# A fused norm and quantised convolution: the weight load moves to ScalarE's queue, and the store of image 0 moves to SyncE's

## The chip, the cores and the metric

The kernel runs on one core of one Trainium2 chip. The metric is the device time of one execution in microseconds (us), as the median of several runs. A core has five engines that matter here: TensorE (PE in the profile), VectorE (DVE), ScalarE (ACT), GpSimd (POOL) and SyncE (SP), which only issues transfers in this kernel. Sixteen DMA engines move data between HBM and the on-chip memory SBUF. Transfers are issued from two places, SP and ACT, and each of the two has its own DMA queue: q1 in the profile is SP's, q10 is ACT's.

## What is computed

The input `x` has 32 images of 512 channels and 28 by 28 pixels in float32, 1.6 MB each. Each image is normalised per group of 16 channels (32 groups), quantised to 16 levels, multiplied with a quantised weight matrix per convolution group (four groups of 128 channels, permuted by one group), passed through an affine step and a ReLU, and added to both the normalised image and the image itself:

```python
def _L0_conv_ref(x, weight, lW, uW, lA, uA, gamma, beta, running_mean, running_var):
    identity = x
    xg = x.reshape(B, G, Cg, H, W)[:, perm]                 # perm = 1, 2, 3, 0
    xa = jnp.clip((xg - lA) / (uA - lA), 0.0, 1.0)
    xa = ste_round(xa * (ACT_LEVELS - 1)) / (ACT_LEVELS - 1)
    wq = ...                                                # the same for the weights, then (wq - 0.5) * 2
    y = jnp.einsum('bgihw,goi->bgohw', xa, wg).reshape(B, C, H, W)
    inv = gamma / jnp.sqrt(running_var + BN_EPS)
    y = y * inv[...] + (beta - running_mean * inv)[...]
    return jax.nn.relu(y) + identity

x = x + _L0_conv_ref(_gn(x), ...)       # _gn: group norm with 32 groups
```

## The kernel before

One image is one tile of 128 partitions by 4 convolution groups by 784 pixels. `images` is a ring of 12 such tiles (`RING`), and image n lives in slot n % 12 from its load to its store: the result is written over the image, and the store goes out from the same slot. So image n can only be loaded when the store of image n - 12 has landed, which the semaphores `stored[j]` tell.

The engines share an image as follows. DVE takes the statistics of two or three of its groups (line 460), ACT those of the rest (lines 236 and 242). PE averages them over the channels of a norm group, POOL makes the coefficients, ACT and POOL write the quantised levels (lines 270 and 424), DVE caps them (line 475), PE multiplies (line 604), POOL (and ACT for the last four images) applies the affine step to the image (lines 413 and 278), and DVE adds the product to it (`finish`, line 482), one group at a time. Each `finish` raises the semaphore `final` by one, so image n is ready for its store at 4n + 4. Statistics run five images ahead of the multiplication (`AHEAD`).

Every engine's program is written out by hand, in order. What bears on transfers:

- SP (line 188 on) loads image 0 in four pieces of one group each (392.0 KB), then the weights `w_raw`, then image 1 in four pieces, then images 2 to 31 whole. From image 12 on each load waits for `stored[j]` (line 198). After that it stores image 30, and image 31 in four pieces.
- ACT (line 218 on) issues two small loads of parameters at the start, and in its main loop the stores of images 0 to 29 (`store`, line 259), each at a fixed place among its activations. The store of image 0 stands behind the four quantisations and the copy of the mean that follow the statistics of image 5.
- DVE waits for `weights_in` (line 511) behind the statistics of image 0, then prepares the weights (lines 512 to 519), and only then takes the statistics of image 1.

Of the kernel before, what the change touches and what calls it, by code (L numbers as in the profile page):

```python
# [12 lines left out]
P = 128  # L13
# [6 lines left out]
RING = 12  # L20
PARTS = 3
AHEAD = 5
SINGLE = 2
HELPED = 4
ACT_STORES = 30
SETS = 3
SUBSETS = 4
DMA = 16


def fused_norm_quantised_conv(nc, x, weight, limits, channel_params, out):

    B, C, H, W = x.shape
# [44 lines left out]
    def output_group(g):  # L78
        return (g + G - 1) % G

    with ExitStack() as ctx:
        def sb(name, shape, dtype):
            return ctx.enter_context(nc.sbuf_tensor(name, shape, dtype))
# [4 lines left out]
        def sem(name):  # L88
            return ctx.enter_context(nc.semaphore(name))
# [25 lines left out]
        w_raw = sb("w_raw", [P, G, P], F32)  # L115
# [30 lines left out]
        weights_in = sem("weights_in")  # L146
# [40 lines left out]
        @block.sync  # L187
        def _(sync):
            for n in range(SINGLE):
                for g in (0, G - 1, 1, 2):  # L190
                    sync.dma_start(images[:, n, g], x_v[n][:, g]).then_inc(first_loaded[n][g], DMA)
                if n == 0:
                    sync.dma_start(w_raw[:], weight.rearrange("(g o) i -> o g i", o=P)).then_inc(weights_in, DMA)

            def load(n):
                j = n % RING
                if n >= RING:
                    sync.wait_ge(stored[j], DMA * (n // RING))
                sync.dma_start(images[:, j], x_v[n]).then_inc(x_loaded[j], DMA)

            def store(n):
                sync.wait_ge(final, G * n + G)
                sync.dma_start(out_v[n], images[:, n % RING]).then_inc(stored[n % RING], DMA)

            for n in range(SINGLE, B):
                load(n)
            for n in range(ACT_STORES, B - 1):
                store(n)
            for g in range(G):
                o = output_group(g)  # L210
                sync.wait_ge(final, G * (B - 1) + g + 1)
                sync.dma_start(out_v[B - 1][:, o], images[:, (B - 1) % RING, o]).then_inc(stored[(B - 1) % RING], DMA)
            for j in range(RING):
                stores = len(range(j, B, RING)) + (G - 1 if j == (B - 1) % RING else 0)
                sync.wait_ge(stored[j], DMA * stores)

        @block.scalar
        def _(act):
            act.dma_start(rows[:], channel_params.rearrange("k (g p) -> (k g) p", p=P)).then_inc(rows_in, DMA)
            act.dma_start(limit_row[:], limits).then_inc(limits_in, DMA)  # L220
            act.wait_ge(eps_done, 1)
            nc.scalar.activation(early[:], eps[:, 0:1], ACT.Sqrt, bias=eps[:, 1:2])
            act.wait_ge(cols_turned, 1)
# [33 lines left out]
                nc.scalar.activation(std[:], var_ps[:, 0:2 * G], ACT.Sqrt, bias=eps[:, 0:1]).then_inc(std_done, 1)  # L257

            def store(n):
                if 0 <= n < ACT_STORES:  # L260
                    act.wait_ge(final, G * n + G)
                    act.dma_start(out_v[n], images[:, n % RING]).then_inc(stored[n % RING], DMA)

# [38 lines left out]
            for n in range(-1, B - 1):  # L302
                m = n + AHEAD
                if n % 2:
                    u = (n + 3) // 2
                    for g in range(quant_on_act(n + 2) if n + 2 < B else 0):
                        quantise(n + 2, g)
                        if g == 0 and u < PAIRS:
                            copy_mean(u)
                    store(n - 1)  # L310
                    if m < B:
                        image_sums(m)
                    if u < PAIRS:
                        deviation(u)
                    if m < B:
                        image_squares(m)
                    for g in range(G - affine_on_act(n + 1), G):
                        affine(n + 1, g)
                else:
                    for g in range(G - affine_on_act(n + 1), G):  # L320
                        affine(n + 1, g)
                    if m < B:
                        image_stats(m)
                    store(n - 1)
                    for g in range(quant_on_act(n + 2) if n + 2 < B else 0):
                        quantise(n + 2, g)
# [329 lines left out]
```

## Time and profile before

| | us |
|---|---|
| median of three runs | 258.81 (258.80 to 259.05) |
| the profiled execution, its own time | 258.41 |
| the span that its profile shows | 256.7 |
| DVE, ACT, POOL and PE busy | 230.0, 215.2, 212.0, 193.9 |

The span runs from the first to the last record of the profile; 1.7 us of the execution lie outside it. The page of the profile gives the busy time of each engine, and, in 40 slices of the span, how busy the DMA engines were and how many GB/s they moved. The views used further on are: the busy times by stretch (with the mean rate of the DMA engines), the DMA view (what each queue moved in a stretch, and how long the transfers issued there took to land), the instructions in order of time, and the waits. In the views in order of time, `SPq` and `ACTq` are the sequencers that issue transfers; a long duration there means that the issue was held up.

### The profile page before, as it was taken

To read this page: it belongs to the slowest core of one execution; us is meant where nothing else is said; L and a number is where in the kernel's file an instruction comes from. 1 tells how busy PE (TensorE), PEld (TensorE's weight loads), DVE (VectorE), ACT (ScalarE), POOL (GpSimd) and SP (SyncE) were. 2 spreads that over 40 slices of the span, in tenths; PEclk is the share of its full clock that TensorE was granted. 3 is DMA by queue.
4 is the path that set the end of the run, shared out by engine and by line. 5 is a ranking of instruction groups with operands and counts; after the bars stand their busy time and mean duration, and the time that the engine had idled before them with its cause. 6 is when DMAs were issued, how large, how long until landed. Compare 5 with 4: busy or idle time off the path is not lost.

```text
span 256.7 us, 3463 instructions
## 1 busy us (share of the span) xinstructions
PE 193.9 (76%) x999; PEld 109.3 (43%) x999; DVE 230.0 (90%) x363; ACT 215.2 (84%) x394; POOL 212.0 (83%) x340
## 2 busy tenths in 40 slices
PE   1142996969889888979797997877696969889920
PEld 0132644435454444445443554343444435454510
DVE  2898698999999999999999899999999999969940
ACT  4437898999999999989999889999899888999300
POOL 6126869999999999999999999999999999999100
PEclk9999999797979798988979599999979797979995
DMA  6999999999999999999999999999999999999994
GB/s 225 398 411 411 408 409 406 418 416 417 418 414 418 417 416 418 411 418 416 416 415 416 418 416 413 419 417 415 417 413 418 416 418 409 402 400 402 393 399 193
DMA packets 34516, 103.25 MB, mean 402 GB/s; under 512 B 1202, under 2 KB 1730, under 8 KB 34498
## 3 DMA queue, kind: packets, MB, share of 16 engines
q1 hardware_dynamic: 18624, 54.86, 53.8%
q10 hardware_dynamic: 15874, 48.18, 47.0%
q8 instruction: 8, 0.13, 0.2%
q14 instruction: 10, 0.08, 0.1%
HBM read 51.65 MB, written 51.38 MB: 401 GB/s over the span
## 4 chain that ended last, share of the span: by engine, by line
POOL 52%; DVE 16%; issue 11%; PE 9%; ACT 5%; DMA 2%; DVEq 0%; SPq 0%; POOLq 0%; ACTq 0%
POOL images L413 27%; POOL levels L424 8%; DVE images L482 7%; PE prod L604 6%; DVE stats L460 4%; POOL dev L375 3%; DVE codes L475 3%; PE var_ps L584 3%; POOL dev L378 2%; DMA images<-in_x 2%; POOL scaled L404 2%; ACT levels L270 2%; POOL coef L406 2%; POOL norm L402 1%; ACT unused L242 1%
## 5 line engine op out<-in xcount | busy, mean ns | idle before, releaser
L604 PE MATMUL prod<-codes,w_t 128*128 128x392 bf16 x768 | 160.8, 369 | 7.9 <-DVE codes L475 2.9
L482 DVE SCALAR_TENSOR_TENSOR images<-prod,floor,images 128x784 f32<-128x784 f32 x128 | 128.0, 1019 | 8.5 <-PE prod L604 8.2
L413 POOL TENSOR_SCALAR images<-images,coef 128x784 f32<-128x784 f32 x120 | 123.7, 1042 | 0.0
L604 PEld LDWEIGHTS prod<-codes,w_t 128*128 128x128 bf16 x768 | 79.1, 110 | 81.6 <-issue 24.6
L270 ACT ACTIVATE levels<-images,coef 128x784 int16<-128x784 f32 x95 | 91.3, 1028 | 1.1 <-issue 1.1
L460 DVE BATCH_NORM_STATS2 stats<-images 128x6 f32<-128x392 f32 x136 | 68.9, 551 | 5.4 <-DMA images<-in_x 5.4
L236 ACT ACTIVATE unused<-images 128x784 bf16<-128x784 f32 x60 | 50.7, 847 | 7.5 <-DMA images<-in_x 5.2
L242 ACT ACTIVATE unused<-images,sums 128x784 bf16<-128x784 f32 x60 | 56.1, 939 | 0.1
L475 DVE TENSOR_SCALAR codes<-levels 128x3136 bf16<-128x3136 int16 x32 | 34.7, 1085 | 1.0 <-ACT levels L270 0.7
L584 PE MATMUL var_ps<-dev,avg 128*128 128x8 f32 x128 | 19.6, 280 | 20.0 <-POOL dev L382 20.0
L424 POOL TENSOR_SCALAR levels<-images,coef 128x784 int16<-128x784 f32 x33 | 33.6, 1020 | 0.1
L584 PEld LDWEIGHTS var_ps<-dev,avg 128*128 128x128 f32 x128 | 18.6, 221 | 25.4 <-POOL dev L382 25.2
L375 POOL TENSOR_TENSOR dev<-stats,gmean 128x16 f32<-128x16 f32 (+1 forms) x16 | 10.9, 682 | 9.6 <-ACT gmean L250 9.6
L575 PE MATMUL mean_ps<-sums,avg 128*128 128x4 f32 (+1 forms) x32 | 6.5, 274 | 12.2 <-DVE sums L468 12.2
L575 PEld LDWEIGHTS mean_ps<-sums,avg 128*128 128x128 f32 x32 | 5.2, 203 | 17.2 <-DVE sums L468 12.2
L242 ACT ACTIVATION_READ_ACCUMULATOR unused<-images,sums 128x1 f32 x60 | 11.4, 190 | 0.0
L236 ACT ACTIVATION_READ_ACCUMULATOR unused<-images 128x1 f32 x60 | 11.3, 188 | 0.0
L256 ACT ACTIVATE half_var<-var_ps,eps 128x8 f32<-128x8 f32 x16 | 4.2, 265 | 6.7 <-PE var_ps L584 6.4
L398 POOL TENSOR_TENSOR newt<-rough 128x8 f32<-128x8 f32 x16 | 3.9, 242 | 5.5 <-DVE rough L492 5.5
L250 ACT ACTIVATE gmean<-mean_ps 128x8 f32<-128x8 f32 x16 | 2.7, 170 | 6.1 <-PE mean_ps L576 6.0
L278 ACT ACTIVATE images<-images,coef 128x784 f32<-128x784 f32 x8 | 7.7, 1032 | 0.0
L404 POOL TENSOR_TENSOR scaled<-norm,coef_mul 128x32 f32<-128x32 f32 x16 | 6.5, 409 | 1.2
(66 smaller groups left out, 83.2 us busy)
## 6 DMA issues: line engine op xcount, KB each, us to landing
images<-in_x SPq DMA_DIRECT2D x30, 1568.0 KB, 14.5
out<-images ACTq DMA_DIRECT2D x30, 1568.0 KB, 18.8
images<-in_x SPq DMA_DIRECT2D x8, 392.0 KB, 6.6
out<-images SPq DMA_DIRECT2D x1, 1568.0 KB, 8.8
out<-images SPq DMA_DIRECT2D x4, 392.0 KB, 7.4
w_raw<-in_weight SPq DMA_DIRECT2D x1, 256.0 KB, 6.5
rows<-in_channel_params ACTq DMA_DIRECT2D x1, 8.0 KB, 2.3
limit_row<-in_limits ACTq DMA_DIRECT2D x1, 0.0 KB
```

The lines of the kernel that those rows point to most:

```text
L236: nc.scalar.activation(unused[:, g % 2], images[:, n % RING, g], ACT.Identity, scale=1.0 / HW, accum_out=sums[:, u % 2, 0, j, g:g + 1]).th ...
L242: nc.scalar.activation(unused[:, g % 2], images[:, n % RING, g], ACT.Square, scale=-1.0, bias=sums[:, u % 2, 0, j, g:g + 1], accum_out=sum ...
L270: nc.scalar.activation(levels[:, n % 2, g], images[:, n % RING, g], ACT.Relu, bias=coef[:, u % 2, 1, 0, G * j + g:G * j + g + 1], scale=co ...
L375: nc.gpsimd.tensor_tensor(dev[:, :, 0:k], stats[:, par, :, 0:k, :, 1], mean[:, :, 0:k].to_broadcast([P, 2, k, SUBSETS]), ALU.subtract)
L413: nc.gpsimd.tensor_scalar(here, here, coef[:, u % 2, 0, 1, G * j + o:G * j + o + 1], coef[:, u % 2, 1, 1, G * j + o:G * j + o + 1], ALU.mu ...
L424: nc.gpsimd.tensor_scalar(levels[:, n % 2, g], images[:, n % RING, g], coef[:, u % 2, 0, 0, G * j + g:G * j + g + 1], coef[:, u % 2, 1, 0, ...
L460: nc.vector.bn_stats(two, images[:, n % RING, g, h * HALF:(h + 1) * HALF]).then_inc(bn_done, 1)
L475: nc.vector.tensor_scalar(codes[:, n % 2], levels[:, n % 2], 0.0, TOP, ALU.max, ALU.min).then_inc(capped, 1)
L482: nc.vector.scalar_tensor_tensor(out=two, in0=prod[:, k % SETS, :, 0:HALF], scalar=floor[:, o:o + 1], in1=two, op0=ALU.max, op1=ALU.add).t ...
L575: nc.tensor.matmul(mean[:, :, 0:k], avg[:], sums[:, par, 0, :, 0:k], start=True, stop=True)
L584: done = nc.tensor.matmul(var, avg[:], dev2[:, :, :, s], start=False, stop=(s == SUBSETS - 1))
L604: done = nc.tensor.matmul(prod[:, k % SETS, h, 0:HALF], w_t[:, part, output_group(g)], codes[:, n % 2, g, h * HALF:(h + 1) * HALF], start= ...
```

## The change

Two transfers change their place.

- The load of the weights leaves SP's program, where it stood between the four pieces of image 0 and the four of image 1. It becomes the third transfer that ACT issues, ahead of ACT's first activation.
- The store of image 0 leaves ACT's loop. SP issues it, behind the load of image 11 and ahead of the load of image 12, which is the first that waits for this very store.

```diff
@@ block.sync
             for n in range(SINGLE):
                 for g in (0, G - 1, 1, 2):
                     sync.dma_start(images[:, n, g], x_v[n][:, g]).then_inc(first_loaded[n][g], DMA)
-                if n == 0:
-                    sync.dma_start(w_raw[:], weight.rearrange("(g o) i -> o g i", o=P)).then_inc(weights_in, DMA)
...
-            for n in range(SINGLE, B):
+            for n in range(SINGLE, RING):
+                load(n)
+            store(0)
+            for n in range(RING, B):
                 load(n)
             for n in range(ACT_STORES, B - 1):
                 store(n)
@@ block.scalar
             act.dma_start(limit_row[:], limits).then_inc(limits_in, DMA)
+            act.dma_start(w_raw[:], weight.rearrange("(g o) i -> o g i", o=P)).then_inc(weights_in, DMA)
             act.wait_ge(eps_done, 1)
...
             def store(n):
-                if 0 <= n < ACT_STORES:
+                if 0 < n < ACT_STORES:
                     act.wait_ge(final, G * n + G)
```

SP's program from its start, before. `images<-in_x` of 128x784 is one group of an image, of 128x4x784 a whole image; `stored0` is the semaphore of slot 0.

```order
L191 DMA images<-in_x 128x784 x4
L193 DMA w_raw<-in_weight 128x4x128
L191 DMA images<-in_x 128x784 x4
L199 DMA images<-in_x 128x4x784 x10
L199 DMA images<-in_x 128x4x784 [waits stored0]
L199 DMA images<-in_x 128x4x784 [waits stored1]
```

The same place after:

```order
L191 DMA images<-in_x 128x784 x8
L197 DMA images<-in_x 128x4x784 x10
L201 DMA out<-images 128x4x784 [waits final]
L197 DMA images<-in_x 128x4x784 [waits stored0]
L197 DMA images<-in_x 128x4x784 [waits stored1]
```

The weights are gone from between images 0 and 1, and a store that waits for `final` stands between the ten unconditional loads and the first load that waits for a slot.

ACT's program around the first two stores, before (images 6 and 7 are those whose loads it waits for):

```order
L250 ACTIVATE gmean<-mean_ps 128x8 [waits coef_done,mean_done]
L270 ACTIVATE levels<-images,coef 128x784 x2
L262 DMA out<-images 128x4x784 [waits final]
L236 ACTIVATE unused,sums<-images 128x784 [waits dev_done,var_done,squared,x_loaded6]
```

and after:

```order
L252 ACTIVATE gmean<-mean_ps 128x8 [waits coef_done,mean_done]
L272 ACTIVATE levels<-images,coef 128x784 x2
L238 ACTIVATE unused,sums<-images 128x784 [waits dev_done,var_done,squared,x_loaded6]
```

The store of image 0 with its wait is gone from there, and ACT's first store is now that of image 1, at its old place behind the statistics of image 7.

## Rows read from the trace of the kernel before

**Rows 1.** The page: the engines, the DMA engines in 40 slices, HBM traffic.

```profile
PE 193.9 (76%) x999; PEld 109.3 (43%) x999; DVE 230.0 (90%) x363; ACT 215.2 (84%) x394; POOL 212.0 (83%) x340
...
DMA  6999999999999999999999999999999999999994
GB/s 225 398 411 411 408 409 406 418 416 417 418 414 418 417 416 418 411 418 416 416 415 416 418 416 413 419 417 415 417 413 418 416 418 409 402 400 402 393 399 193
...
HBM read 51.65 MB, written 51.38 MB: 401 GB/s over the span
```

**Rows 2.** Busy time of each engine by stretch; the last column is the DMA rate.

```profile
4.00:6.50 2.50, 0.69 (x3) 0.60 (x3) 1.82 (x9) 1.24 (x4) 1.30 (x3) 1.00 0.96 306
8.00:40.00 32.00, 18.43 (x79) 12.37 (x79) 27.58 (x57) 22.48 (x43) 16.74 (x31) 1.00 1.03 410
45.00:60.00 15.00, 12.99 (x69) 7.21 (x68) 14.97 (x24) 14.47 (x30) 14.45 (x22) 0.86 1.03 417
60.00:200.00 140.00, 118.56 (x622) 65.57 (x620) 136.31 (x211) 133.37 (x251) 133.99 (x201) 0.89 1.03 416
216.00:240.00 24.00, 21.63 (x118) 11.72 (x117) 21.74 (x28) 23.21 (x33) 21.43 (x31) 0.92 1.03 402
240.00:248.00 8.00, 4.99 (x30) 2.53 (x27) 6.93 (x8) 0.00 (x0) 0.00 (x0) 1.00 1.01 392
```

**Rows 3.** DMA view, 40.2 to 43.7: what each queue moved.

```profile
q1 hardware_dynamic: 464, 1.41, 102.0%
q8 instruction: 1, 0.02, 1.9%
```

**Rows 4.** DMA view, 62 to 200: what each queue moved.

```profile
q10 hardware_dynamic: 9473, 28.81, 51.9%
q1 hardware_dynamic: 9372, 28.49, 51.2%
```

**Rows 5.** In order of time: SP's issues (start, duration, line, count).

```profile
2.64 0.43 SPq L193 DMA_DIRECT2D w_raw<-in_weight  x1
...
5.85 31.53 SPq L199 DMA_DIRECT2D images<-in_x  x10
...
33.52 3.86 SPq L199 DMA_DIRECT2D images<-in_x  x1
...
53.13 0.37 SPq L199 DMA_DIRECT2D images<-in_x  x1
...
60.76 0.37 SPq L199 DMA_DIRECT2D images<-in_x  x1
...
200.81 0.37 SPq L199 DMA_DIRECT2D images<-in_x  x1
```

**Rows 6.** Waits of SP's queue: us in total, times, longest.

```profile
SPq L199 <- DMA out<-images: 156.1, 20, 15.7
SPq L203 <- DVE images L482: 42.0, 1, 42.0
```

**Rows 7.** In order of time: ACT's issues of stores 0, 1, 2, 3.

```profile
40.18 0.42 ACTq L262 DMA_DIRECT2D out<-images  x1
...
49.01 0.40 ACTq L262 DMA_DIRECT2D out<-images  x1
...
54.47 0.38 ACTq L262 DMA_DIRECT2D out<-images  x1
...
62.82 0.38 ACTq L262 DMA_DIRECT2D out<-images  x1
```

**Rows 8.** DMA view: issued in 36 to 44 (load 11, store 0), size, us to landing.

```profile
images<-in_x SPq DMA_DIRECT2D x1, 1568.0 KB, 26.8
out<-images ACTq DMA_DIRECT2D x1, 1568.0 KB, 12.9
```

**Rows 9.** DMA view: load 31, issued at 200.81.

```profile
images<-in_x SPq DMA_DIRECT2D x1, 1568.0 KB, 13.7
```

**Rows 10.** In order of time, the start: DVE and ACT behind the first loads.

```profile
7.32 2.07 DVE L460 BATCH_NORM_STATS2 stats<-images 128x6 f32<-128x392 f32 x4 [1.41 <-DMA images<-in_x]
9.31 0.53 DVE L512 TENSOR_SCALAR w_rest<-w_raw,cols,w_rng 128x512 f32<-128x512 f32 x1
12.05 2.90 DVE L460 BATCH_NORM_STATS2 stats<-images 128x6 f32<-128x392 f32 x6
...
17.08 0.86 ACT L236 ACTIVATE unused<-images 128x784 bf16<-128x784 f32 x1 [0.54 <-DMA images<-in_x]
...
21.00 0.86 ACT L236 ACTIVATE unused<-images 128x784 bf16<-128x784 f32 x1 [0.47 <-DMA images<-in_x]
...
36.03 1.03 DVE L482 SCALAR_TENSOR_TENSOR images<-prod,floor,images 128x784 f32<-128x784 f32 x1
```

**Rows 11.** In order of time, the end: ACT's issues and image 31, DVE's last group.

```profile
208.40 3.91 ACTq L262 DMA_DIRECT2D out<-images  x1
...
212.49 0.86 ACT L236 ACTIVATE unused<-images 128x784 bf16<-128x784 f32 x1 [1.05 <-issue]
...
216.54 0.86 ACT L236 ACTIVATE unused<-images 128x784 bf16<-128x784 f32 x1
...
241.20 5.73 DVE L482 SCALAR_TENSOR_TENSOR images<-prod,floor,images 128x784 f32<-128x784 f32 x6
```

**Rows 12.** DMA view, 248 to 256.7: rate in 40 slices, and the last piece stored.

```profile
GB/s 418 389 418 389 404 418 361 433 389 433 361 418 404 389 375 418 433 404 332 317 332 288 274 245 187 144 144 58 87 58 58 14 29 29 0 0 0 0 0 0
...
out<-images SPq DMA_DIRECT2D x1, 392.0 KB, 8.8
```

## The prediction

> **What bounds the kernel now.** I read the page first, and on it the line of the DMA engines: they are 90% busy or more in every slice but the first and the last, at about 400 to 419 GB/s [rows 1]. DVE is 90% busy too, ACT and POOL a little less, so the next question is which of the two would be missed. The DMA view answers it: the last piece of image 31 is issued at about 247, right behind DVE's last group (241.20 + 5.73 = 246.9) [rows 11], and takes 8.8 us to land, with the DMA engines at their full rate until about 252 [rows 12]. So a queue of stores, some 5 us deep, stands between the last computed group and the end. The bytes are the same before and after (51.65 MB read, 51.38 MB written [rows 1]). The time is therefore start + bytes / rate + tail, and a change to the order of transfers counts only through the rate, through an idle stretch of the DMA engines, or through compute that comes more than the depth of that queue later.
>
> The table by stretch shows that the rate has levels [rows 2]: 410 GB/s while only loads run (8 to 40), 416 to 417 while loads and stores run side by side (45 to 200), 402 while only stores run (216 to 240). In the side by side stretch the two queues share evenly: 9,473 packets of ACT's against 9,372 of SP's [rows 4]. So what I have to work out is how many images are moved in each of the three manners.
>
> **The change, part 1: the weights.** They cost the same bytes on either queue. On SP the issue takes 0.43 us [rows 5], but SP is far ahead of the DMA engines (it is soon held up at its issues: 31.5 us for the ten loads from 5.85 on [rows 5]), so those 0.43 us buy nothing. On ACT they delay its first activation by about as much; ACT has nothing to do before image 0's second piece, so that is free. What moves is the order of arrival. The weights now share with the pieces of image 0, instead of coming behind them. 0.26 MB at 410 GB/s are 0.64 us, so the pieces that DVE waits for at 7.32 come by 0 to 0.64 us later, and its preparation of the weights (9.31) and the statistics of image 1 (12.05) follow [rows 10]: DVE was without a gap from 7.32 on, so nothing absorbs it. It could also be less than nothing if the weights came long before 9.31 and DVE's wait at 7.32 were unchanged, but then the pieces still have to be worked off in the same order. I take +0.6 us for the computation. On the path that sets the end this is worth 0: the 5 us of queued stores hide it, less about 2 us that a last piece needs by itself (1 us of transfer, 392 KB at 402 GB/s, and an allowance of 1 us to start), so 3 us of cover. If that cover were gone, the 0.6 us would count in full.
>
> **Part 2: the store of image 0.** Before, ACT issues it at 40.18 [rows 7], though its last group was finished at 37.06 (36.03 + 1.03) [rows 10]. Until 43.7 ACT's queue moves nothing [rows 3]; then it shares with loads. It lands at 53.1 (40.2 + 12.9 [rows 8]), and SP, which had waited for it for 15.7 us [rows 6], issues load 12 at 53.13 [rows 5]. After, SP comes to this store when it is done with issuing load 11, at 33.52 + 3.86 = 37.4 [rows 5], finds it ready (or within the 0.6 us of part 1), and puts it **behind** loads 9, 10 and 11 in the same queue. So an earlier issue gives a later transfer. Loads come every 3.92 us while they are alone (images 2 and 3 at 17.08 and 21.00 [rows 10]), so load 11 now lands at 21.0 + 8 x 3.92 = 52.4, where before it landed at 60.3 (33.5 + 26.8 [rows 5, 8]). Only then come stores, and meanwhile ACT has issued store 1 (49.0) and soon store 2 (54.5), both at their old places [rows 7]. Store 0 and store 1 share the engines: two images at 402 GB/s are 8.0 us, so store 0 lands at about 60.5, 7 us later than before. Load 12 goes out then, and load 13 right behind it (before: 60.76 [rows 5]). With the allowance of 1 us to start and some for landing, loads and stores run side by side again from about 62. Until then store 2 keeps the engines at work: stores 0, 1 and 2 are 12 us of work from 52.4 on, to 64.4. So I count no idle stretch.
>
> Now the three manners. Before: loads alone until 43.7, which leaves (52.4 - 43.7) / 3.92 = 2.2 images; 9.8 are loaded alone, 22.2 side by side with as many stores, and 9.8 are stored alone. That fits the trace: load 31 lands at 200.8 + 13.7 = 214.5 [rows 5, 9], and 9.8 x 3.99 us more give 253.6. After: 12 are loaded alone, 20 side by side; stored alone are 32 - 20 = 12 (2.4 of them between 52.4 and 62, 9.6 at the end). So 2.2 pairs leave the fast manner for the two slow ones. One image is 1.606 MB, 2.2 are 3.53 MB, and they cost 3.53 x (1/410 + 1/402 - 2/416) ms per GB = **+0.42 us**. With the ends of the slices on the page that are of one manner (406 to 411 for loads, 400 to 403 for stores, 415 to 417 beside each other) this is 0.3 to 0.6 us. It could be below nothing only if the DMA engines lost something in the shared stretch that they don't lose alone, and the rates say the opposite.
>
> A rule of the Trainium skill ("DMA: Bandwidth & Descriptors", section "Issuing engines are not separate DMA queues") says that transfers started on several engines run on the same 16 DMA engines and interleave, so that more issuers save only the time of issuing. By that rule alone the whole change would be worth nothing.
>
> **Part 3: what the later loads do to the computation.** 20 pairs at 7.72 us (3.21 MB at 416 GB/s) from 62 on bring load 31 at 216.4, 1.9 us later than before. ACT took image 31 at 216.54 [rows 11], 2.0 us after it landed, and itself comes 0.6 us later now. Here a stall of ACT may shrink as well: it stood for 1.05 us before 212.49 because a store's issue was held up for 3.91 us [rows 11]. I count 0, and at most 1 us, under the 3 us of cover. Early in the run there is no need of image 12 for a long time after 70.
>
> **The sum.** 258.41 (this execution's own time) + 0.42 + 0 + 0 = 258.83. The profiled execution is 0.40 us under the median of the three runs, 258.81; on the median's scale that is 259.23, and I say 259.2. For a verdict, 0.2% is about what a measurement of this kernel can tell from no change, which is 0.52 us: below 258.29 is faster, above 259.33 slower. The forecast lies just inside the upper edge.
>
> **Rivals.**
>
> *Rate levels that don't follow the manner.* The 402 of the end and the 410 of the start may belong to those parts of the run (the ring being filled, the last images) rather than to loads or stores being alone. Then the moved pairs cost nothing: 258.8, the same. For it: all of the rows for one manner are from one end of the run. Against it: the rate goes up within the 20 us around 43.7, and down just where load 31 has landed [rows 1, 2]. The rule of the Trainium skill above would give this time. Chance 0.18.
>
> *The DMA engines run dry around 62 (slower).* SP stands in line for the store of image 0, and loads 12 and 13 with it, 7 us longer than before. As long as ACT's stores 1 and 2 are in the queue, nobody misses them. It decides if store 0 lands after about 63.4, or if store 2 is issued later than about 60 in place of 54.5: from there each us is lost in full, since the bytes are still to be moved. The same wait makes all later loads late; from 5 us on (2.0 of slack at image 31, 3 of cover) the computation too would reach the end. The place where I can be off is store 0's landing, which I have from two images of work; an uneven split of the engines of 2 to 3 us would bring it about. Price some 1 to 1.5 us: 260.3. Chance 0.15.
>
> *The start or the end gets better (faster).* From 4.0 to 6.5 the engines moved only 306 GB/s, though 96% busy [rows 2]. That costs 2.5 x (1 - 306 / 410) = 0.63 us against the stretch after. If this comes from eight small loads and the weights on one queue, the move could give it back. And from 240 to 248 the rate is 392 in place of 402, 0.2 us, because stores came a little late there; an ACT that is held up less could fill that. Both together against the cost: 259.23 - 0.83 = 258.4, and with the first rival's rates 258.0. Against it: the weights came only behind the slow stretch (issued at 2.64, used at 9.31 [rows 5, 10]), so they can hardly be its cause. Chance 0.17, of which 0.12 under 258.29.
>
> *That the change doesn't do what it says* is no case by itself: by my count the store of image 0 is indeed not sooner, and that is in the forecast.
>
> **How the numbers follow.** Forecast 0.50, from 258.8 to 259.8 by the bounds 0.3 to 0.6 and the scatter of the runs (258.80 to 259.05); 0.30 of it under 259.33 and 0.20 over. With the rivals: faster 0.12, same 0.30 + 0.18 + 0.05 = 0.53, slower 0.20 + 0.15 = 0.35. The range goes from 258.3, where only the faster case is left out, to 260.3.
>
> **What the profile after would show.** SP's store of image 0 issued near 37.4 to 41 and landing near 60.5; ACT's queue empty until about 50; load 12 issued at about 60.5 and load 13 right behind; two stretches of stores alone, 52 to 62 near 402 GB/s and again from about 216; load 31 landing near 216; image 1's statistics on DVE at about 12.6. I am wrong in the size if the rate in 52 to 62 is 410 or more, wrong in the mechanism if store 0 shares with loads before 50, and the slower rival holds if a slice near 62 falls under 390. If the end moves with the computation and not with the bytes, then the 3 us of cover were a misreading.

## The result and the profile after

The change makes the kernel slower: median 260.34 us of 22 runs against 258.72 us for 22 runs of the kernel before taken beside them. The ratio is 1.0052, with a 95% interval of 1.0041 to 1.0062, so about +1.35 us (1.1 to 1.6). On the scale of the 258.81 us shown ahead of the prediction this is 260.2. The two medians lie 1.6 us apart, a little more than the ratio on record gives; all prices below go by such ratios and their intervals. The spans of the two profiled executions, 258.8 and 256.7 us, lie 2.1 us apart. Of all runs of the experiments one, of 343.9 us (e6), was in a slow state and is left out.

The page after, its parts 1 and 2, to be read against [rows 1]:

```profile
PE 195.6 (76%) x999; PEld 110.8 (43%) x999; DVE 228.2 (88%) x363; ACT 215.1 (83%) x394; POOL 212.6 (82%) x340
...
DMA  6999999999999999999999999999999999999995
GB/s 225 399 413 412 409 410 407 406 401 319 382 416 414 417 417 416 415 416 417 418 414 416 417 418 417 415 417 416 415 414 417 418 414 412 401 399 401 399 400 210
...
HBM read 51.65 MB, written 51.38 MB: 398 GB/s over the span
```

The bytes are the same. The first seven slices and those from the twelfth on differ by 4 GB/s at most, but for the 38th and the last, which are fuller than before. The eighth and ninth (406 and 401 in place of 418 and 416) show what was forecast, loads alone and then stores alone. The tenth and the eleventh do not: 319 GB/s where it had 417, and 382 where it had 418. The share of busy time of the DMA engines, as a digit, hides this: it is 9 in both. The table by stretch for the same kernel places the loss (columns as in [rows 2], the DMA share and rate last):

```profile
58.00:60.00 2.00, 1.89 (x15) 1.46 (x15) 2.00 (x3) 1.75 (x3) 1.60 (x5) 1.00 0.73 282
62.00:64.00 2.00, 1.71 (x10) 0.60 (x7) 2.00 (x4) 2.00 (x6) 1.95 (x2) 1.00 0.97 256
64.00:67.00 3.00, 1.20 (x7) 0.54 (x8) 3.00 (x6) 2.91 (x9) 2.26 (x7) 1.00 1.03 414
68.00:76.00 8.00, 6.06 (x37) 3.64 (x38) 7.97 (x13) 7.85 (x14) 7.92 (x10) 0.97 1.02 387
216.00:240.00 24.00, 22.48 (x119) 12.60 (x120) 22.87 (x32) 21.78 (x35) 22.34 (x35) 0.87 1.03 402
240.00:248.00 8.00, 7.51 (x45) 3.97 (x42) 8.00 (x10) 3.87 (x5) 2.93 (x4) 1.00 1.03 398
```

At 58 to 60 the DMA engines really lack work (share 0.73, 282 GB/s). At 62 to 64 they are busy and move only 256 GB/s. Against 401 (stores alone), 409 and 416 GB/s this is 2 x 0.30 = 0.6 us, 2 x 0.37 = 0.75 us, and 8 x 0.07 = 0.56 us from 68 to 76: 1.9 us in these three stretches. The DMA view of 40 to 80 gives the whole loss in bytes, the kernel before first:

```profile
DMA packets 5440, 16.61 MB, mean 415 GB/s; under 512 B 154, under 2 KB 154, under 8 KB 5437
DMA packets 5104, 15.58 MB, mean 390 GB/s; under 512 B 146, under 2 KB 146, under 8 KB 5101
```

1.03 MB are missing, which is 2.5 us at 416 GB/s, the forecast's own term among them. Up to 40 us and from 80 to 216 us both kernels move the same to within 0.02 MB. The end, on the other hand, is a little fuller than before: 398 in 240 to 248, where [rows 2] had 392. So the span is 2.1 us longer.

What led there, in order of time. The start on DVE, which stands against [rows 10], and the issue of the weights:

```profile
1.79 0.40 ACTq L222 DMA_DIRECT2D w_raw<-in_weight  x1
...
8.98 1.04 DVE L462 BATCH_NORM_STATS2 stats<-images 128x6 f32<-128x392 f32 x2 [0.17 <-DMA images<-in_x]
11.37 0.55 DVE L514 TENSOR_SCALAR w_rest<-w_raw,cols,w_rng 128x512 f32<-128x512 f32 x1 [1.35 <-DMA w_raw<-in_weight]
11.95 0.43 DVE L515 TENSOR_SCALAR w_rest<-w_rest 128x512 f32<-128x512 f32 x1
...
14.13 1.96 DVE L462 BATCH_NORM_STATS2 stats<-images 128x6 f32<-128x392 f32 x4
```

The weights are issued 0.85 us earlier and are used at 11.37 in place of 9.31: DVE waits for them for 1.35 us. The statistics of image 1 begin at 14.13 in place of 12.05, so the computation is 2.1 us late. About 0.6 us of that comes from the pieces of image 0 (DVE is done with them at 10.0 in place of 9.4), the rest from the wait for the weights. The DMA view gives the transfer itself 9.6 us to land, where it had 6.5:

```profile
w_raw<-in_weight ACTq DMA_DIRECT2D x1, 256.0 KB, 9.6
```

Then the stores. SP's issues of store 0, of load 12 and of load 13, and ACT's of stores 1 and 2 (against [rows 5, 7]):

```profile
39.42 2.96 SPq L201 DMA_DIRECT2D out<-images  x1
...
58.83 0.37 SPq L197 DMA_DIRECT2D images<-in_x  x1
...
61.45 0.37 SPq L197 DMA_DIRECT2D images<-in_x  x1
```

```profile
51.85 0.41 ACTq L264 DMA_DIRECT2D out<-images  x1
58.26 0.39 ACTq L264 DMA_DIRECT2D out<-images  x1
```

Store 0 takes 19.4 us to land, at 58.8, and load 12 goes out at 58.83, 5.7 us later than before. Store 2 goes out at 58.26, 3.8 us later than before. From about 54 on each queue has one store to work off, store 0 on SP's and store 1 on ACT's. The DMA view of 57 to 58 and of 58 to 60 shows how they run out (packets, MB, and the time that the packets took as a share of the 16 engines'):

```profile
q10 hardware_dynamic: 124, 0.39, 99.9%
q1 hardware_dynamic: 4, 0.01, 3.3%
...
q10 hardware_dynamic: 193, 0.56, 72.6%
q1 hardware_dynamic: 2, 0.00, 0.4%
```

Nearly all of store 0 has been moved by 57, but load 12 waits for its last packets until 58.8. The DMA engines that are through with stores 0 and 1 have nothing to do in the meantime. Load 12 doesn't move at once when it is issued either: from 58.9 to 62.5 SP's queue moves no packet.

### The profile page after: what moved, and what is told of

Its sections match the earlier page's. It is cut to its first block, busy times and chain, and to the rows that moved or that the text cites. A ratio compares the mean times of both kernels' runs of the same rounds, so it can differ in the third digit from the quotient of the medians.

```text
span 258.8 us, 3463 instructions
## 1 busy us (share of the span) xinstructions
PE 195.6 (76%) x999; PEld 110.8 (43%) x999; DVE 228.2 (88%) x363; ACT 215.1 (83%) x394; POOL 212.6 (82%) x340
## 4 chain that ended last, share of the span: by engine, by line
POOL 43%; DVE 26%; PE 12%; issue 11%; DMA 4%; DVEq 0%; ACTq 0%; ACT 0%; POOLq 0%
POOL images L415 22%; DVE images L484 13%; PE prod L606 8%; POOL levels L426 7%; DVE stats L462 6%; DVE codes L477 5%; PE var_ps L586 4%; DMA w_raw<-in_weight 4%; POOL dev L380 3%; POOL dev L377 2%; POOL coef L408 2%; POOL newt L400 1%; POOL dev L384 1%; POOL scaled L406 1%; POOL newt L401 1%
## 5 line engine op out<-in xcount | busy, mean ns | idle before, releaser
L415 POOL TENSOR_SCALAR images<-images,coef 128x784 f32<-128x784 f32 x120 | 129.7, 1091 | 0.0
L477 DVE TENSOR_SCALAR codes<-levels 128x3136 bf16<-128x3136 int16 x32 | 32.9, 1027 | 0.7 <-ACT levels L272 0.4
L426 POOL TENSOR_SCALAR levels<-images,coef 128x784 int16<-128x784 f32 x33 | 32.7, 993 | 0.1
L586 PE MATMUL var_ps<-dev,avg 128*128 128x8 f32 x128 | 21.2, 293 | 13.8 <-POOL dev L384 13.8
L586 PEld LDWEIGHTS var_ps<-dev,avg 128*128 128x128 f32 x128 | 20.7, 242 | 18.2 <-POOL dev L384 17.8
L377 POOL TENSOR_TENSOR dev<-stats,gmean 128x16 f32<-128x16 f32 (+1 forms) x16 | 7.3, 457 | 12.4 <-ACT gmean L252 12.4
L380 POOL TENSOR_TENSOR dev<-sums,gmean 128x16 f32<-128x16 f32 (+1 forms) x16 | 8.7, 542 | 0.0
L613 PE MATMUL prod<-ident,w_raw 128*128 128x128 f32 x4 | 1.1, 434 | 9.5 <-DVE w_raw L520 9.5
```

The lines of the kernel that those rows point to most:

```text
L377: nc.gpsimd.tensor_tensor(dev[:, :, 0:k], stats[:, par, :, 0:k, :, 1], mean[:, :, 0:k].to_broadcast([P, 2, k, SUBSETS]), ALU.subtract)
L380: nc.gpsimd.tensor_tensor(dev[:, :, k:G], own[:, :, k:G].to_broadcast([P, 2, G - k, SUBSETS]), mean[:, :, k:G].to_broadcast([P, 2, G - k, ...
L415: nc.gpsimd.tensor_scalar(here, here, coef[:, u % 2, 0, 1, G * j + o:G * j + o + 1], coef[:, u % 2, 1, 1, G * j + o:G * j + o + 1], ALU.mu ...
L426: nc.gpsimd.tensor_scalar(levels[:, n % 2, g], images[:, n % RING, g], coef[:, u % 2, 0, 0, G * j + g:G * j + g + 1], coef[:, u % 2, 1, 0, ...
L477: nc.vector.tensor_scalar(codes[:, n % 2], levels[:, n % 2], 0.0, TOP, ALU.max, ALU.min).then_inc(capped, 1)
L586: done = nc.tensor.matmul(var, avg[:], dev2[:, :, :, s], start=False, stop=(s == SUBSETS - 1))
```

## The experiments

Each kernel was timed beside the kernel before on the same chip; ratios are to those runs. One count of 0.1% is 0.26 us.

**One half at a time.** e1 has the weights on ACT's queue and the store of image 0 at its old place:

```diff
-                if n == 0:
-                    sync.dma_start(w_raw[:], ...).then_inc(weights_in, DMA)
...
             act.dma_start(limit_row[:], limits).then_inc(limits_in, DMA)
+            act.dma_start(w_raw[:], ...).then_inc(weights_in, DMA)
```

> Half of the change: the weights on ScalarE's queue, the store of image 0 where it was. Theory (two parts that need each other): the weights land late (11.3 in place of 9.1), so the whole computation comes 2 to 3 us later, but the queue of stores at the end covers it, and stores mix with loads from about 46: 258.7 to 259.3, +0.0 to +0.5 us on before. The DMA rate has no slice under 400 in the middle. Rival (the late weights cost by themselves, because the end follows the computation): +1.3 us or more, near the full change.

Measured: 259.17 us, ratio 1.0027 (1.0006 to 1.0048), +0.7 us. The middle value is above the +0.0 to +0.5 expected, but the interval (0.2 to 1.2) takes in much of that range; the rival's +1.3 lies just outside. There is no gap in the middle (412 GB/s in 45 to 60, 416 from 60 to 200); most of the loss is near the end:

```profile
230.00:240.00 10.00, 9.72 (x49) 4.95 (x49) 7.91 (x10) 9.82 (x13) 9.35 (x15) 0.85 0.96 374
240.00:248.00 8.00, 7.12 (x42) 3.98 (x43) 8.00 (x10) 3.65 (x4) 2.17 (x2) 1.00 0.88 342
```

e2 has only the store on SP, behind load 11:

```diff
-            for n in range(SINGLE, B):
+            for n in range(SINGLE, RING):
+                load(n)
+            store(0)
+            for n in range(RING, B):
                 load(n)
...
-                if 0 <= n < ACT_STORES:
+                if 0 < n < ACT_STORES:
```

> The other half: the store of image 0 on SyncE behind load 11, the weights where they were. Theory: computation in time, store 2 issued at about 54.5, so the DMA engines have work until load 12 comes; the only cost is that about two pairs of load and store no longer run side by side: +0.3 to +0.6 us on before, and no slice near 60 under 390 GB/s. Rival (the store behind the loads drains the DMA engines by itself): +1.3 us or more and a slice near 320 GB/s at 58 to 62, as in the full change.

Measured: 259.50 us, ratio 1.0042 (1.0024 to 1.0061), +1.1 us. By the middle values the store is the larger half, though the intervals of e1 and e2 overlap, and it costs more than twice my term for it. The interval (0.6 to 1.6) doesn't leave out the rival's +1.3. The profiled run of e2 is its fastest (258.79 of 258.79 to 260.79), and it has no dip: 401 GB/s at 58 to 60, 409 at 62 to 64, 406 at 64 to 67. So this one run looks as I had forecast, and the other nine are slower.

**Is it the delay that the weights bring, or their packets?** e3 is e2, and e5 the kernel before, each with DVE's first operation on the weights repeated:

```diff
             dve.wait_ge(weights_in, DMA)
-            chained(nc.vector.tensor_scalar(w_rest[:], w_raw[:], bounds[:, 0:1], w_rng[:, 1:2], ALU.subtract, ALU.mult))
+            for _ in range(5):
+                chained(nc.vector.tensor_scalar(w_rest[:], w_raw[:], bounds[:, 0:1], w_rng[:, 1:2], ALU.subtract, ALU.mult))
```

> The store on SyncE as in the change, weights at their old place, and VectorE's first operation on the weights done five times in place of once (the same values; 4 x 0.55 = 2.2 us more ahead of the statistics of image 1). Theory: what the weights' new place does is to delay the computation, nothing else, so this gives the full change's time, +1.2 to +2 us on before, store 2 is issued near 57 to 58 and the DMA engines have a slice of 320 to 360 GB/s near 58 to 60. Rival (the weights' packets on the other queue cost DMA time or disturb the order of the engines): the time of the store alone, +0.3 to +0.6.

> The kernel before, both transfers at their old places, with VectorE's first operation on the weights done five times in place of once: 2.2 us of delay to the computation and nothing else. The weights alone on ScalarE's queue (e1) gave +0.7 us. Theory (late weights act through the delay of the computation alone, and the stores queued at the end cover less than I had counted): the same, +0.4 to +1.2 us, with slices of 350 to 390 GB/s among the last five. Rival (3 us of cover hold, and e1's loss is from the weights' packets): no change, the last slices at 400.

Measured: e3 260.29 us, ratio 1.0066 (1.0046 to 1.0086); e5 259.12 us, ratio 1.0022 (1.0005 to 1.0040). The delay in the place of the weights' move gives what the move gives: e5 beside e1 (1.0022 and 1.0027), e3 beside the full change (1.0066 and 1.0052), within the intervals. In e3 store 2 went out at 57.41, as expected, but the slow stretch came at 62 to 64 (351 GB/s) and not at 58 to 60 (400). e5 loses at the end as e1 does:

```profile
230.00:240.00 10.00, 9.93 (x49) 5.01 (x49) 7.71 (x10) 9.86 (x13) 9.53 (x15) 0.83 0.96 375
240.00:248.00 8.00, 7.04 (x42) 3.94 (x43) 8.00 (x10) 3.60 (x4) 2.25 (x2) 1.00 0.88 343
```

374 and 375, 342 and 343: the same picture at the end, which speaks for the weights acting through the late computation. In the middle the two runs differ: e5 has 375 and 358 GB/s at 60 to 64, where e1 has 412 and 416. How late the computation is at the end, DVE's last groups tell (before 241.20 [rows 11]; here after the change, in e1 and in e5):

```profile
243.71 5.73 DVE L484 SCALAR_TENSOR_TENSOR images<-prod,floor,images 128x784 f32<-128x784 f32 x6
244.90 5.73 DVE L481 SCALAR_TENSOR_TENSOR images<-prod,floor,images 128x784 f32<-128x784 f32 x6
244.98 5.73 DVE L482 SCALAR_TENSOR_TENSOR images<-prod,floor,images 128x784 f32<-128x784 f32 x6
```

In e1 and e5 image 1's statistics began 2.9 and 2.7 us late (14.90 and 14.72), and the last groups 3.7 and 3.8 us late. That is more than the 3 us of cover that I had counted, and it is over by about what the runs cost, 0.7 and 0.6 us. After the change it is 2.5 us, and there the end is full. So these runs don't refute 3 us of cover. The DMA engines do lose 10 x (1 - 375 / 402) + 8 x (1 - 343 / 402) = 1.8 us of work on average from 230 to 248, and the end moves by 0.6. That would fit engines of unequal progress, of which those ahead run dry while the last one still has stores queued. This reading is an inference; the view doesn't tell the engines apart.

**Do the rates follow the manner?** e4 computes nothing; it moves `x` through the 12 tiles to the output in phases, so its output is `x`: loads alone, stores alone, loads alone again, then both together, then the last stores.

> No computation at all, only transfers of x through the ring of 12 tiles to the output (the output is x): 12 loads alone, 12 stores alone, 12 loads alone, then 12 stores beside 8 loads, and the last 8 stores. Theory (the rate follows the manner): about 410 GB/s in both stretches of loads alone, 402 in the stores alone in the middle of the run, 416 side by side. Rival (the rate follows the part of the run): the middle stretches all at 416, or all the same.

Measured (264.62 us; here columns are stretch, POOL, clock, DMA share, rate):

```profile
8.00:45.00 37.00, 0.00 (x0) 1.00 1.03 411
60.00:96.00 36.00, 0.00 (x0) 1.00 1.03 404
108.00:145.00 37.00, 0.00 (x0) 1.00 1.03 411
172.00:210.00 38.00, 0.00 (x0) 1.00 1.03 418
222.00:250.00 28.00, 0.00 (x0) 1.00 1.03 404
```

Loads alone 411 at the start and in the middle, stores alone 404 in the middle and at the end, together 418. The rate follows the manner and not the part of the run: the first rival of the prediction is out. It isn't a matter of two queues being at work either: after the change, from 53 to 57, both queues carry stores alone (278 packets of ACT's, 250 of SP's) at 402 GB/s.

**How much of it is the computation?** In e6, e7 and e8, DVE's statistics of images 8 to 31 read 56 columns in place of 392, so the output rests on a part of the data; DVE has much less to do from 57 us on, and nothing changes ahead of that. e6 is the kernel before, e7 is e2, e8 the full change.

```diff
-                nc.vector.bn_stats(two, images[:, n % RING, g, h * HALF:(h + 1) * HALF]).then_inc(bn_done, 1)
+                cols_read = 56 if n >= 8 else HALF
+                nc.vector.bn_stats(two, images[:, n % RING, g, h * HALF:h * HALF + cols_read]).then_inc(bn_done, 1)
```

> The kernel before with VectorE's statistics of images 8 to 31 read over 56 columns in place of 392 (so these statistics, and the output, are of a part of the data): about 40 us less work on VectorE from 57 us on, nothing changed ahead of that. Theory: the kernel before is bound by the transfers, with up to 0.3 us lost at the end where stores come late: -0.2 to -0.8 us. Rival (the computation bounds it): several us faster.

> The store of image 0 on SyncE (as e2), with the same light statistics from image 8 on. Against e6 this is the price of the store's new place in the transfers alone, since the end can't be held up by the computation. Theory: +0.3 to +0.6 us on e6, from two pairs less side by side. Rival (part of e2's +1.1 us is a late computation at the end): if e7 is +1.1 us on e6 as well, it is not.

> The full change with the same light statistics from image 8 on. Against e7: what the late weights do to the transfers, by way of the stretch at 58 to 60 in which the DMA engines run dry (319 GB/s in that slice of the full change), the end being covered. Theory: the bytes not moved there are lost, +0.8 to +1.6 us on e7. Rival (what is lost there is only time that fast DMA engines would have waited at the end anyway): within 0.4 us of e7.

| | median | ratio to before | interval |
|---|---|---|---|
| e6, before with light DVE | 258.94 | 0.9998 | 0.9985 to 1.0011 |
| e7, store on SP with light DVE | 259.89 | 1.0040 | 1.0023 to 1.0056 |
| e8, full change with light DVE | 259.90 | 1.0035 | 1.0020 to 1.0050 |

e6 shows that DVE doesn't bound the kernel before: with much less work it gives nothing that can be told, where 0.2 to 0.8 us had been expected. Together with e4, which has the same rates without any computation, it leaves the transfers as the bound. e7 against e6 is 0.42%, as e2 against before and more than the +0.3 to +0.6 us expected: the store's price needs no late computation at the end. e8 against e7 is nothing, against my expectation of +0.8 to +1.6. But e8 says less about late weights than it was meant to. In its profiled run they took 8.0 us to land and image 1's statistics began at 12.61, 0.8 us after e7's and not 2; store 1 went out at 49.58, as in e7 (49.56). How late the weights were in the other eleven runs isn't known.

Whether the two parts add in the full change can't be told from these runs: e1 and e2 make 0.69% together, e3 0.66%, the full change 0.52%, with intervals of 0.1 to 0.2 each. Where each run loses, the bytes moved by stretch show (MB):

| profiled run | 0 to 40 | 40 to 80 | 80 to 216 | 216 to 248 |
|---|---|---|---|---|
| before | 15.13 | 16.61 | 56.59 | 12.78 |
| after | 15.14 | 15.58 | 56.61 | 12.83 |
| e1, weights only | 14.94 | 16.47 | 56.60 | 12.09 |
| e2, store only | 15.12 | 16.35 | 56.61 | 12.74 |
| e3, store and delay | 15.02 | 16.07 | 56.60 | 12.30 |
| e5, delay alone | 15.05 | 16.30 | 56.60 | 12.11 |
| e7, store, light DVE | 15.05 | 15.88 | 56.59 | 12.87 |
| e9, store before load 10 | 15.02 | 16.52 | 56.61 | 12.76 |

0.1 MB is 0.24 us. The late computation costs at the end (e1, e3, e5) and also in the middle (e5 against before, e3 against e2), probably because ACT's stores come later with it. The profiled run of the full change loses everything in the middle.

The profiled run of e7 (260.34 us) shows the dip that e2's lacked:

```profile
58.00:60.00 2.00, 2.00 (x14) 1.15 (x14) 2.00 (x5) 2.00 (x7) 2.00 (x3) 1.00 1.03 401
62.00:64.00 2.00, 1.34 (x9) 0.57 (x7) 2.00 (x3) 2.00 (x5) 1.69 (x5) 1.00 1.00 325
64.00:67.00 3.00, 1.76 (x11) 0.83 (x10) 2.94 (x10) 3.00 (x6) 2.92 (x5) 1.00 1.00 344
```

Here the computation is in time and the engines are not idle; yet 325 and 344 GB/s in five us cost 2 x 0.20 + 3 x 0.16 = 0.9 us. The kernel e6 has 419 and 418 in the same two stretches. One thing that differs between e2 and e7 is when load 12 goes out, which waits for the last packets of store 0 (10 packets of SP's queue beside 307 of ACT's, from 59 to 61.4 in e7). Its issue in e2 and in e7:

```profile
59.22 0.37 SPq L199 DMA_DIRECT2D images<-in_x  x1
```

```profile
61.41 0.37 SPq L199 DMA_DIRECT2D images<-in_x  x1
```

e8's run lies between (load 12 at 60.52, then 354 and 366 GB/s). That is an order of three runs and not a cause: in both e2 and e7 the stores work on without a gap until 62 and the first packets of load 12 move only then. Nor is the slow stretch tied to the store's place. e5, with both transfers where they were, has one at 60 to 64, and there it is store 2 (issued at 58.84) that begins again on an empty queue. Why packets move slowly at such a moment while the engines count as busy is left open.

**Is it SP, or the place behind the loads?** e9 is e2 with the store two loads sooner.

```diff
-            for n in range(SINGLE, B):
+            for n in range(SINGLE, 10):
+                load(n)
+            store(0)
+            for n in range(10, B):
                 load(n)
```

> The store of image 0 on SyncE again, weights at their old place, but two loads earlier: behind the load of image 9 and ahead of that of image 10. SyncE then waits some 12 us for image 0 to be finished (37.1), with loads 7 to 9 still queued. Theory (the cost is that the store lands behind loads 10 and 11, at about 60, so load 12 comes late and the DMA engines lose rate between 62 and 68): the store lands near 50, load 12 goes out near 50, loads and stores run side by side from about 50, no slice under 400 GB/s between 50 and 75, and the time is that of before, -0.2 to +0.4 us. Rival (any store on SyncE's queue costs, since the two queues then don't share): +0.8 us or more, as e2.

Measured: 259.16 us, ratio 1.0016 (1.0001 to 1.0032), +0.4 us. SP issued it as soon as image 0 was finished, and it landed at 48.7:

```profile
37.12 0.39 SPq L203 DMA_DIRECT2D out<-images  x1
37.55 11.60 SPq L199 DMA_DIRECT2D images<-in_x  x3
```

```profile
54.00:68.00 14.00, 11.18 (x67) 6.01 (x64) 13.97 (x23) 13.05 (x26) 12.84 (x20) 1.00 1.03 417
```

No dip. All the same, loads and stores run side by side only from about 53, after 12 images loaded alone: as many pairs are missing as in the change, and +0.4 us is what 3.53 MB at the slower rates come to (0.42). So e9 fits the forecast's term by itself, with an interval too wide (0.0 to 0.8 us) to confirm its size. e2's middle value is 0.26% or 0.7 us higher, and what e9 lacks of it is the wait of load 12 for store 0 and the slow stretch behind it; the intervals of e2 and e9, measured on two chips, still overlap a little. That any store on SP's queue costs as much as e2 is not borne out: the +0.8 us of that rival lies at the very edge of the interval.

**Other places.** e10 stores image 0 from ACT, but behind the first of the four quantisations:

```diff
                         quantise(n + 2, g)
+                        if g == 0 and n == 1:
+                            store(0)
...
-                    store(n - 1)
+                    if n > 1:
+                        store(n - 1)
```

> The kernel before with the store of image 0 on ScalarE three activations sooner: behind the first quantisation of image 3 (about 37.4) in place of behind all four and the copy of a mean (40.2). Theory: loads and stores run side by side from about 41 in place of 43.7; that is 0.7 pairs more in the fast manner, worth 0.1 to 0.2 us: not to be told from no change, -0.4 to +0.2. Rival (ScalarE waits for the store's semaphore and delays the quantisations): +0.3 or more.

Measured: 258.96 us, ratio 1.0005 (0.9991 to 1.0018): no difference that can be told. e11 makes the weights ACT's first transfer:

```diff
-                if n == 0:
-                    sync.dma_start(w_raw[:], ...).then_inc(weights_in, DMA)
...
+            act.dma_start(w_raw[:], ...).then_inc(weights_in, DMA)
             act.dma_start(rows[:], ...).then_inc(rows_in, DMA)
             act.dma_start(limit_row[:], limits).then_inc(limits_in, DMA)
```

> The weights as ScalarE's first transfer (at 0.8 us), ahead of its two small loads, the store of image 0 at its old place. Theory (on ScalarE's queue the small packets of the weights take turns with the packets of the images, and on one or two of the 16 engines they trail, so that the whole lands at 11.3): issued 1 us earlier they still share with image 0, land at 8 to 10, and VectorE takes the statistics of image 1 at 12 to 13: +0 to +0.6 us on before. The parameters behind them come later, which moves VectorE's range operations by 1 to 3 us, beside its wait for image 0. Rival (the queue as such makes them late): 11 us again and +0.7.

Measured: 258.39 us, ratio 0.9992 (0.9976 to 1.0008). The weights, issued at 0.8 and so 1 us sooner than in the change, land after 4.2 us in place of 9.6, far sooner than I expected, and from 4.0 to 6.5 the rate is nearly that of loads alone:

```profile
4.00:6.50 2.50, 0.22 (x1) 0.18 (x1) 1.04 (x2) 0.00 (x0) 0.01 (x1) 1.00 1.05 398
```

398 GB/s where [rows 2] had 306. A part of the slow stretch has only moved: from 2 to 4 e11 has 267 GB/s where the kernel before had 341, and by 40 us it is 0.12 MB ahead. DVE is later all the same (image 1 at 12.79 in place of 12.05), since the parameters now come behind the weights. e12 puts e10 and e11 together:

> e11 and e10 together: the weights as ScalarE's first transfer, and the store of image 0 on ScalarE behind the first quantisation of image 3. Theory: e11's start (some 0.3 us ahead in the transfers by image 8) and 0.7 pairs more side by side (0.1 us): -0.2 to -0.5 us on before, an interval that may just leave out no change. Rival (both gains are eaten by a computation that is 0.7 us late at the start): 0.0 to +0.3.

Measured: 258.45 us against 259.01, ratio 0.9976 (0.9964 to 0.9988), -0.6 us (0.3 to 0.9), a little more than the 0.2 to 0.5 expected. This version beats both kernels, by little.

## Why the prediction was right or wrong, point by point

The range (258.3 to 260.3) held the time, and the direction of the shift was right, but the forecast itself, 259.2, was 1 us too low, and "same" was the likeliest verdict where the measured one is slower. The range held only because it had been stretched to the price of a rival. The mechanism of the "slower" rival, to which I gave 0.15, is the one that took place, at its place and near its price (260.3). The sign named for it, a slice near 62 under 390 GB/s, is there (319 and 382).

- **What bounds the kernel: right.** e6 takes work off DVE and gains nothing, and e4 has the same rates with no computation. The bytes are the same, and the rate decides.
- **The rate levels: right.** e4 shows 411, 404 and 418 out of their place in the run, and e9 fits the term: +0.42 worked out, +0.41 measured. With an interval of 0.03 to 0.8 so close a match is luck.
- **Part 1, the weights: wrong in size.** I took 0.6 us of delay from their bytes. The pieces of image 0 came later by about that, but DVE was 2.1 us late in all, because it then waited for the weights, which took 9.6 us and not 6.5 to land. I also let the delay reach the end as it was at the start; in e1 and e5 it grew from 2.9 and 2.7 us to 3.7 and 3.8. The 3 us of cover are not refuted by that: the end moved by 0.7 and 0.6 us. But the cover is no sharp edge. In e12, whose last groups are only 1.4 us late, 240 to 248 already runs at 364 GB/s, and the kernel has the lowest ratio all the same. My term of 0 for part 1 also left out the main thing, that late computation makes ACT's stores late: store 2 at 58.26 in place of the 54.5 that part 2 takes for granted.
- **Part 2, the store: the mechanism was right, the sum too small.** Store 0 went behind loads 9 to 11, ACT's queue stayed empty till 51.85, load 12 waited until 58.83 (I had said 60.5), loads and stores met again from about 62.5. That last time came out by luck: load 12 was issued 1.7 us sooner than I had said and then moved no packet for 3.7 us, where I had allowed 1. The failed step is "so I count no idle stretch". I added 12 us of work from 52.4 on as if it were one queue that never runs out, with store 2 in it from 54.5. Store 2 came only at 58.26, load 12 waited for the last packets of store 0, and in 58 to 60 the engines had work for 0.73 of the time. Slow stretches followed while they were busy. I had put both at nothing; from 40 to 80 us 1.03 MB or 2.5 us went missing in this run. With the computation in time (e2, e7) the store's term of +0.42 measured +1.1. The profiled runs of these two have no idle stretch; e7's has the slow packets, whose cause stays open.
- **The decision point of the slower rival was wrong**: I let it begin with store 0 landing after 63.4 or store 2 after 60. It began at 58.8 and 58.26.
- **Part 3: right.** ACT took image 31 at 219.15 without a wait; late loads didn't stop the computation.
- **The faster rival: its mechanism exists, but this change doesn't reach it.** After the change 4.0 to 6.5 runs at 302 GB/s, as before at 306. With the weights issued first (e11, e12) it runs at 398, but a stretch before it is slower. I had argued that the weights come only behind the slow stretch and can hardly be its cause; their place in the queues does bear on it. e4, with neither weights nor parameters and with whole images from the start, has 416 there.
- **The rule of the Trainium skill** ("DMA: Bandwidth & Descriptors", section "Issuing engines are not separate DMA queues"), by which the change is worth nothing: the two queues do share the same engines, evenly in [rows 4], but the traces disagree that only the time of issuing is at stake. Moving a store changes how long loads run beside stores, at 418 GB/s against 411 and 404 (e4), and a store that goes behind loads in one queue takes 19.4 us to land and holds up the load that waits for it.

Still open: why the packets move slowly at 4.0 to 6.5 and at 62 to 67, why load 12 moved no packet for 3.7 us, and why the weights took 8.0 to 10.3 us from 1.8 and 4.2 from 0.8. In e1 and in e5 3 of 12 runs are 1 us or more above the median; what tells these runs from the others I don't know. With one profile of each kernel, where a run loses is known for that run alone.

## What to carry to other kernels

In a kernel bound by its transfers, count the images moved in each manner (loads alone, stores alone, both), and price the difference; then look at the one load that waits for one store, since it waits for the last few packets while most engines are through. A store moved behind all the loads of the busy queue is issued sooner and lands later (37.16 and 59.22 in e2, 40.18 and 53.1 before); two loads sooner in the same queue it landed at 48.7 (e9). And add what a delay does to the issue of the stores that are to fill the gap. "The engines are 9 tenths busy" is not enough in such a stretch: look at the GB/s.

## What was not expected of the hardware

- The 256 KB of weights landed in 9.6 us when they were ACT's third transfer (1.79) and in 4.2 us as its first (0.8), beside the same loads of image 0.
- DMA engines counted as busy (share 0.97 to 1.00) moved 256, 325 and 344 GB/s about the time when loads began again on an empty queue, against 418 with both queues full. In e5 it was 358 when stores began again.
- Load 12, issued at 58.83 on an empty queue, moved its first packet after 62.5; in e7, issued at 61.41, it did so by 62.5, within about 1 us.
- 2.7 us of delay at the start of the computation (e5) cost 0.6 us, in a kernel whose DVE could lose much of its work and gain nothing (e6): a bound by transfers and a price for late computation go together.
